# Weight rows of the first two experts spread by TensorE, with the requests and VectorE's first turn rewritten around it

## The reference

```
scores = sigmoid(x @ router_w.T)
topk_idx = the 8 best of scores + e_bias, within the 4 best of 8 groups
w = scores at topk_idx;  w = w / (w.sum(-1) + 1e-20) * 2.5
coef = zeros(T, 64).at[token, topk_idx].add(w)
g = einsum('th,ehi->tei', x, Wg);  u = einsum('th,ehi->tei', x, Wu)
moe_out = einsum('tei,eih->th', silu(g) * u * coef[:, :, None], Wd)
shared = silu(x @ SWg) * (x @ SWu) @ SWd
out = x + moe_out + shared
```

## Time and profile before

| | |
|---|---|
| three runs | 663.19 us median (662.78 to 667.07) |
| profiled execution | 664.93 us |
| its span, first to last instruction | 663.3 us |
| mean granted TensorE clock | 0.974 |
| TensorE matmul, busy | 618.9 us (93%) |
| TensorE weight load, busy | 502.8 us (76%) |
| VectorE, ScalarE, GpSimd busy | 382.7, 402.7, 305.4 us |

### The profile page before, as it was taken

One profiled execution on the slowest core, in us unless ns is written; L12 is line 12 of the kernel. 1 busy time (PEld: TensorE's weight loads), 2 busy tenths in 40 slices (PEclk: granted clock), 3 DMA queues, 4 the chain that ended last, 5 costly groups with the idle time before them and its releaser, 6 DMA issues.

```text
span 663.3 us, 15407 instructions
## 1 busy us (share of the span) xinstructions
PE 618.9 (93%) x4808; PEld 502.8 (76%) x4809; DVE 382.7 (58%) x1205; ACT 402.7 (61%) x973; POOL 305.4 (46%) x486
## 2 busy tenths in 40 slices
PE   7999899999988999998999989999899799999996
PEld 6998566666677999876878756666656798999995
DVE  2533667777761111138898755666576466666663
ACT  4545899989953443245767697786551455555553
POOL 4223555558645000011010003777415688888883
PEclk9999999999968999999999999999998799999998
DMA  6138700005343995112120020000034867677744
GB/s 161 51 96 276 265 2 2 2 2 194 108 138 108 309 326 170 32 37 81 36 57 2 1 54 2 1 1 1 2 99 95 228 185 185 180 187 194 194 114 115
DMA packets 71884, 71.20 MB, mean 107 GB/s; under 512 B 10740, under 2 KB 65298, under 8 KB 71702
## 3 DMA queue, kind: packets, MB, share of 16 engines
q1 hardware_dynamic: 63484, 59.62, 29.4%
q0 software_dynamic: 4816, 8.07, 5.8%
q10 hardware_dynamic: 3530, 2.82, 1.5%
HBM read 55.18 MB, written 15.31 MB: 106 GB/s over the span
## 4 chain that ended last, share of the span: by engine, by line
PE 67%; ACT 11%; DVE 8%; issue 5%; DMA 4%; POOL 3%; ACTq 0%; SPq 0%; DVEq 0%; POOLq 0%
PE psum L1399 6%; PE psum L1388 6%; ACT probs L911 4%; PE psum L1890 3%; PE psum L1912 3%; PE psum L1899 3%; PE psum L2541 3%; PE psum L2543 3%; PE psum L2542 3%; PE psum L1938 2%; PE psum L837 2%; PE psum L827 2%; DMA x_rows<-xc_dram,slot_rows 1%; PE psum L1673 1%; POOL probs L977 1%
## 5 line engine op out<-in xcount | busy, mean ns | idle before, releaser
L911 ACT ACTIVATE probs<-probs,negmax 100x361 f32<-100x361 f32 x128 | 68.9, 587 | 10.6 <-POOL probs L977 10.5
L990 DVE TENSOR_SCALAR_CACHE_REDUCE probs<-psum 100x361 f32<-100x361 f32 x128 | 60.6, 530 | 17.2 <-PE psum L827 17.2
L837 PEld LDWEIGHTS psum<-ident,probs 100*128 100x128 f32 (+1 forms) x384 | 38.0, 151 | 25.2 <-issue 16.7
L837 PE MATMUL psum<-ident,probs 100*128 100x100 f32 (+1 forms) x384 | 45.9, 255 | 10.8 <-ACT probsT L919 4.0
L977 POOL TENSOR_SCALAR probs<-probs 100x722 f32<-100x722 f32 x64 | 50.5, 788 | 5.1
L1429 ACT ACTIVATE kT_all<-psum,kT_all 128x128 f32<-128x128 f32 x88 | 25.0, 369 | 42.5 <-PE psum L1388 42.5
L2541 PE MATMUL psum<-xT_high,we_high 128*128 128x400 f32 x128 | 45.6, 357 | 3.4 <-DVE v_all L2794 3.4
L2543 PE MATMUL psum<-xT_high,we_low 128*128 128x400 f32 x128 | 45.1, 352 | 0.0
L2542 PE MATMUL psum<-xT_low,we_high 128*128 128x400 f32 x128 | 45.1, 352 | 0.0
L2712 POOL TENSOR_TENSOR we_low<-v_all,we_high 128x512 fp32r<-128x512 f32 (+1 forms) x34 | 40.0, 1309 | 10.6 <-ACT we_high L2630 10.1
L1388 PEld LDWEIGHTS psum<-kT_all,v_all 128*128 128x128 f32 x352 | 40.6, 192 | 4.9 <-issue 4.6
(11 more groups left out here) (473 smaller groups left out, 1801.7 us busy)
## 6 DMA issues: line engine op xcount, KB each, us to landing
v_all<-in_L_ffn_W_dram SPq DMA_DIRECT2D x16, 1024.0 KB, 5.5
xs_dram<-zeros SPq DMA_DIRECT2D x1, 7424.0 KB, 23.5
kT_all<-coefT_dram SPq DMA_DIRECT2D x16, 400.0 KB, 4.3
v_all<-in_L_ffn_Wg_dram SPq DMA_DIRECT2D x32, 128.0 KB, 2.4
v_all<-in_L_ffn_Wu_dram SPq DMA_DIRECT2D x32, 128.0 KB, 2.9
v_all<-in_L_ffn_Wd_dram SPq DMA_DIRECT2D x32, 128.0 KB, 3.1
ctx_nat<-in_ctx_dram SPq DMA_DIRECT2D x16, 192.0 KB, 2.4
kT_all<-xs_dram ACTq DMA_DIRECT2D x13, 128.0 KB, 3.2
```

The source lines that it names most:

```text
L837: last = nc.tensor.transpose(pT_ps[0:rows[t], t, hh * NQ:(hh + 1) * NQ], probs[:, n % NPB, hh, t * P:t * P + rows[t]], ident[0:NQ, 0:NQ])
L911: last = nc.scalar.activation(row, row, ACT.Exp, bias=negmax[:, n % NPB, hh:hh + 1])
L990: last = nc.vector.tensor_scalar(probs[:, n % NPB, hh, 0:NKV], psum[0:NQ, n % 2 * 2 + hh, 0:NKV], -CLAMP, None, ALU.max, ALU.max, accum_ou ...
```

## The change

1. SyncE no longer loads the two `coef_rows` of the first turn. Instead TensorE multiplies column p of `place`, repeated over 128 columns, with `coefT`: the result has on every partition the weight row of the expert at place p. That is two float32 matmuls of 64 x 400 for each p, into the PSUM banks of the gate and up products. VectorE copies the result for p = 0 to `coef_rows[0]`, ScalarE that for p = 1.
2. The other requests of the first turn are reordered: Wg and Wu of dense expert 1 come before Wd of expert 0.
3. In `dve_route1` the three steps on `weight_sum` move behind `place`, so the list is known earlier.
4. On TensorE all four calls of `down` now stand behind the transposes of `coef`; the six matmuls of zeros are gone and the spreading matmuls stand there.
5. VectorE's first turn is written out ahead of its loop, and in it `find_rows` stands behind the first `hidden`.

```diff
@@ sp_experts1
         load_gate_up(0, dense[0])
         dense.append(sp.value_load(expert_list[0:1, 1:2], min_val=0, max_val=E1 - 1))
+        load_gate_up(1, dense[1])
         load_down(0, dense[0])
...
             load_rank(k, small_at(sp, total, 0, k))
+        load_down(1, dense[1])
+        for k in range(2):
+            load_small(0, k, small_at(sp, total, 0, k))
         sp.wait_ge(coefT_stored, 16)
-        load_coef(0, 0, dense[0])
-        load_gate_up(1, dense[1])
-        load_down(1, dense[1])
-        load_small(0, 0, small_at(sp, total, 0, 0))
-        load_coef(0, 1, dense[1])
-        load_small(0, 1, small_at(sp, total, 0, 1))
@@ pe_shared
         nc.tensor.matmul(r_list_ps, e_col, place[:, :], start=True, stop=True).then_inc(route_sums, 1)
-        down(0, 0)
...
         last.then_inc(route_sums, 1)
-        down(0, 1)
-        for half in range(2):
-            down(1, half)
-        pe.wait_ge(route_taken, 2)
-        for _ in range(6):
-            nc.tensor.matmul(psum[:, 3, 0:D], zeros[:, 0:P], zeros[:, :], start=True, stop=True)
+        for m in range(2):
+            for half in range(2):
+                down(m, half)
+        pe.wait_ge(route_taken, 4)
+        for p in range(2):
+            for half in range(2):
+                last = nc.tensor.matmul(gu_ps[2 * p + half], place[:, p:p + 1].broadcast_to([E1, P]),
+                                        coefT[:, half * HT:(half + 1) * HT], start=True, stop=True)
+            last.then_inc(route_sums, 1)
@@ act_shared, behind the stores of coefT and coef
+        act.wait_ge(route_sums, 7)
+        for half in range(2):
+            nc.scalar.activation(coef_rows[1][:, half * HT:(half + 1) * HT], gu_ps[2 + half], ACT.Copy
+                                 ).then_inc(coef_loaded[1], 8)
@@ pe_experts1
         pe.wait_ge(route_step, 5)
+        for p in range(2):
+            pe.wait_ge(coef_loaded[p], 16)
@@ dve_experts1, ahead of the loop, which now begins at turn 1
+        dve.wait_ge(route_sums, 6)
+        for half in range(2):
+            nc.vector.tensor_copy(coef_rows[0][:, half * HT:(half + 1) * HT], gu_ps[half]).then_inc(coef_loaded[0], 8)
+        hidden(0, 0, 0)
+        find_rows(0)
+        hidden(0, 0, 1)
+        first_small = small_experts(0)
+        for k in range(2):
+            split_small(0, k)
+        second_expert(0, first_small)
```

More of the change, by code:

```diff
@@ L2494, in dve_route1 @@
         step(dve, nc.vector.tensor_tensor(work1, scores1, picked, ALU.mult))
-        step(dve, nc.vector.tensor_reduce(weight_sum[:, :], work1, AX.X, ALU.add))
-        step(dve, nc.vector.tensor_scalar(weight_sum[:, :], weight_sum[:, :], 1e-20, None, ALU.add))
-        step(dve, nc.vector.reciprocal(weight_sum[:, :], weight_sum[:, :]))
         dve.wait_ge(route_sums, 1)
@@ L2507, in dve_route1 @@
         nc.vector.tensor_scalar(place[:, :], iota64, place_at[:, 0:1], None, ALU.is_equal).then_inc(route_step, 1)
[L2508 to L2511, removed]
+        mark(nc.vector.tensor_reduce(weight_sum[:, :], work1, AX.X, ALU.add))
         dve.wait_ge(route_sums, 4)
@@ L2514, in dve_route1 @@
         nc.vector.tensor_copy(expert_list[:, 0:E1], r_list_ps).then_inc(route_step, 1)
+        mark(nc.vector.tensor_reduce(n_pairs[:, 0:2], order[0:1, 0:2, 0:E1], AX.X, ALU.add))
+        marked(dve)
+        some_n, size_n, dense_n, least, pairs_n = (n_pairs[:, k:k + 1] for k in range(5))
+        mark(nc.vector.tensor_scalar(weight_sum[:, :], weight_sum[:, :], 1e-20, None, ALU.add))
+        step(dve, nc.vector.tensor_scalar(dense_n, size_n, some_n, 2.0, ALU.subtract, ALU.mult))
+        mark(nc.vector.reciprocal(weight_sum[:, :], weight_sum[:, :]))
+        step(dve, nc.vector.scalar_tensor_tensor(least, some_n, 2.0, dense_n, ALU.add, ALU.max))
         nc.vector.scalar_tensor_tensor(coef, work1, SCALE2, weight_sum[:, :].unsqueeze(2).broadcast_to([NQ, B, E1]),
@@ L2843, in dve_experts1, with small_experts, second_expert @@
         total = dve.value_load(n_used[0:1, 0:1], min_val=0, max_val=E1)
+        def small_experts(i):
+            return [dve.value_load(expert_list[0:1, bass.ds(small_at(dve, total, i, k), 1)], min_val=0, max_val=E1 - 1)
+                    for k in range(2)]
+        def second_expert(i, small):
+            for half in range(2):
+                hidden(i, 1, half)
+            for k in range(2):
+                rows_low(i, k)
+            last_low(i)
+            for k in range(2):
+                small_hidden(i, k, small[k])
+            for k in range(2):
+                hidden_low(i, k)
+            keep_rows(i)
+        dve.wait_ge(route_sums, 6)
+        for half in range(2):
+            nc.vector.tensor_copy(coef_rows[0][:, half * HT:(half + 1) * HT], gu_ps[half]).then_inc(coef_loaded[0], 8)
[3 more added lines that the diff above has]
+        first_small = small_experts(0)
+        for k in range(2):
+            split_small(0, k)
+        second_expert(0, first_small)
         with dve.Fori(0, E1 // (2 * PAIRS)) as o:
-            with dve.If(2 * PAIRS * o < total):
+            with dve.If(2 * PAIRS * o + 2 < total):
                 with dve.Fori(0, PAIRS) as j:
-                    i = o * PAIRS + j
+                    i = o * PAIRS + j + 1
                     with dve.If(2 * i < total):
                         find_rows(i)
-                        small = [dve.value_load(expert_list[0:1, bass.ds(small_at(dve, total, i, k), 1)], min_val=0,
-                                                max_val=E1 - 1) for k in range(2)]
+                        small = small_experts(i)
                         for k in range(2):
@@ L2854, in dve_experts1 @@
                             split_small(i, k)
[L2855 to L2864, removed]
+                        second_expert(i, small)
         dve.wait_ge(x_loaded[0], 32)
```

## The result

The changed kernel took 667.25 us (median of 20 runs, 663.18 to 670.05), the one before 663.41 beside it (20 runs). The ratio is 1.005 with a 95% interval of 1.0034 to 1.0066: a loss of some 3.3 us. In a later session 12 more runs gave 1.0019 (0.9999 to 1.0039) against 35 of before, a loss of 1.3 us whose interval just reaches no loss at all.

What follows compares the result with a forecast made beforehand. TensorE, busy 93% of the span, was taken as the bound, with a 3.4 us wait and its slow clock costing 5.9 us. A start 6.0 us later, partly given back, left +3.6: 663.2 + 3.6 = 666.8 us, range 662.0 to 670.5.

Steps and rivals of the forecast that it cites:

- The sum: Whole kernel: 3.6 us carried to the start of turn 1, 663.2 + 3.6 = 666.8 us by the median.
- the clock case I had assumed: TensorE's clock low before `down`, rising at 509; low again for 3.4 us in the gate products.
- The list and the requests: First turn: list written 1.1 us earlier, no gain by itself; expert 1's weights requested 6.5 us earlier, 3.4 us wait gone.
- TensorE up to the first turn: `down` behind the transposes, partly at low clock; spreading takes 2.8 us and ends at 515.3 (bounds 514 and 516).
- rival A: TensorE's clock stays high through both new gaps: 663.4 us, no change; chance 0.18.
- From there to the turn: Row copies, rounding and subtraction leave TensorE idle 3.0 us; first turn starts at 518.3 instead of 512.33, +6.0 us.
- B: Cheaper spreading, first turn starting near 512.3, stall and its slow clock gone: 657.3 us, faster; chance 0.07.
- The gate products: 48 matmuls without the stall, 1.5 us extra for low clock; they end at 528.6, +1.2 us.
- C: Clock stays low through the whole of both gate products, which then hide the gather: 670.1 us, slower; chance 0.09.
- VectorE's order: Search behind the first `hidden` delays gather, low parts and expert 1's hidden half; 3.6 us carried to turn 1.
- The price of contention: VectorE's search beside GpSimd's subtractions: priced at 0, at most one subtraction's 0.7 us.
- D: Wait on VectorE's L2794 stays, caused by a small weight's or rank's load: 670.2 us; chance 0.04.

Runs made afterwards that it cites:

- after_3: The changed kernel unchanged, profiled a third time; turn 1 started 41.0 us after the start of VectorE's product of scores and picks; no ratio given.
- before_requests: The kernel before with one edit: Wg and Wu of dense expert 1 requested right behind those of expert 0; ratio to before 0.9951.
- spread_early: The changed kernel with the spreading matmuls moved up behind the first call of `down`, the other three calls behind them; ratio to before 0.9989.
- before_2: The kernel before, unchanged, profiled a second time; turn 1 started 37.9 us after the start of VectorE's product of scores and picks; no ratio given.
- search_first: The changed kernel with `find_rows` of the first turn back ahead of the first `hidden`; ratio to before 1.0039.
- fill_gap: The changed kernel with six zero matmuls behind the spreading only; ratio to before 1.0017.
- fill_both: The changed kernel with four zero matmuls between the list and the transposes and six behind the spreading; ratio to before 1.0004.
- both: The changed kernel with the edits of search_first and spread_early together; ratio to before 0.9995.
- early_fill: spread_early plus ranks requested before both Wd loads, VectorE's register loads and search first, four zero matmuls between list and transposes; ratio to before 0.9965.

## Why the prediction was right

**The sum.** 666.8 was forecast, 667.25 measured, with the sign and the mechanism forecast. That they lie 0.5 us apart is partly luck: +3.6 us was forecast, and the two sessions gave +3.3 and +1.3. In the trace that fell into the clock case I had assumed, after_3, turn 1 stands 41.0 us behind the picks; my working put it at 37.3 + 3.6 = 40.9. The first gate product stands there at 20.3, forecast at 20.4. Behind the gap that trace was not the assumed case: its second low stretch lasted 6.8 us, not 3.4. One slip in the working is worth 0.1 us: at the 0.73 of the earlier trace rows, 4.0 us at the low clock are 5.5 records of `down`, not 5.8.

**The list and the requests.** Right: the list came 3.4 us behind the picks instead of 4.7. That this brings nothing by itself no run tests; TensorE came to its first weights 14 to 17 us later. The wait of 3.4 us went, as forecast. What I did not ask is what this part would bring alone; before_requests answers: a gain of 3.3 us by its ratio, while the whole change loses 3.3 and 1.3. So the rest of the change cost 4.6 to 6.6 us. spread_early gives 2.6 to 3.2 of them back; what the remainder is stays open.

**TensorE up to the first turn.** The spreading took 2.95 us at the high clock (2.8 forecast): 64 rows of input cost what 128 do. The clock was a guess: one fall, with the rise at 509. The traces show all cases, no fall (rival A, the profiled run, 37.6 against its forecast of 37.5), a rise after 3.4 us, and one after 6.8. The first gate product, forecast at 20.4 behind the picks, came at 17.3, 19.0 and 20.3. The rule of the Trainium skill ("TensorE: Matmul & The Clock Gate", "What's actually happening") weighed there is now seen from both sides: with the same gap of 2.0 us in the same kernel the clock stayed high in one trace and fell in two, once inside the gap (4.5 us behind the picks) and once 1.2 us after its end (6.3). Nor was the gap of 1.0 us shown to bring down the clock before: before_2 has the same wait of 1.0 us and no fall there. The same page of the Trainium skill remarks that the count of slow matmuls differs from run to run. No row showed it then; these traces do, with low stretches of 0, 3.4 and 6.8 us ahead of the first gate product of the changed kernel.

**From there to the turn.** 3.0 us forecast, 2.99 to 3.01 in all four traces with that order and no fill (search_first among them). This is the core of the loss, and spread_early shows it by taking it away. B (a hidden start) is excluded.

**The gate products.** Here a step was incomplete: I counted 1.5 us for the low clock behind the gap. The clock fell as forecast, and the delay of VectorE's first product, 1.0 to 1.8 us, is of that size. But fill_gap and fill_both, which keep the clock high, save only 0.0 to 0.7 us up to turn 1, because the search then meets GpSimd's subtractions, a price that I had put at 0. So in the changed kernel the slow clock hid the contention. C, a clock low through both gate products, did not come: of the changed kernel's three traces after_3 had the longest such stretch, 4.6 us of them, and was 0.4 to 0.7 us longer from the first gate product to turn 1 (20.7) than the other two. C's price was not tested.

**VectorE's order.** The waits forecast are there: 1.2 us for `h_low` and small ones for the rows. The search ahead of the first product removes them, but the gain in time is not shown. The price of contention, "at most one subtraction's 0.7 us", was mis-sized: it measured 1.1 us in fill_both, 2.2 in both (4.28 less 2.1) and 2.6 in early_fill (4.69 less 2.1). In the changed kernel itself the search came too late to meet the subtractions, so the sum was spared.

**D** did not come: the small weights and ranks were there in time.

## What to carry to other kernels

If a stage waits for a load, first move the request alone: here one moved request gave 3.3 us, and the larger change, which carried the same move, lost 3.3 and 1.3, in good part because it put the replacement for another load behind 5.6 us of unrelated matmuls and in front of the first weights. Work that makes an operand for another engine goes ahead of the filler, and the filler beside the engine's answer. And look at what a stage depends on after the change: in three traces each, the stage that waited for a load varied by 0.6 us and the one that ran on TensorE's pace by 3.4.

## What the runs showed of the hardware that was not expected

- A VectorE instruction with two SBUF operands (the search, 1.05 us alone) took 2.13 to 3.18 us beside GpSimd's subtractions, and these took 4.84 instead of 3.23. Removing one TensorE delay moved it into that overlap.
- The same gap of TensorE, 2.0 us long in the same program, went with no low stretch, one of 3.4 us or one of 6.8 us, and in four traces the clock fell ahead of it, while TensorE was busy with small matmuls. With zero matmuls in the gaps there was no low stretch in this stage (fill_both, early_fill, one trace each; the run both, without them, had none either).
- A float32 matmul with 64 rows of input ran at the pace of one with 128: 2.95 us for 8 records, 5.56 for 16.
